# Self-attention of layer 3: the exponential ahead of the copies out of PSUM on ScalarE

## The reference

```python
q = jnp.einsum('bsc,hcd->bhsd', xn, wq)
k = jnp.einsum('btc,hcd->bhtd', yn, wk)
v = jnp.einsum('btc,hcd->bhtd', yn, wv)
a = jax.nn.softmax(jnp.einsum('bhsd,bhtd->bhst', q, k) * D ** (-0.5), axis=-1)
if causal:
    s, t = (a.shape[-2], a.shape[-1])
    mask = (jnp.arange(t)[None, :] > jnp.arange(s)[:, None]).astype(a.dtype)
    a = a * mask
o = jnp.einsum('bhst,bhtd->bhsd', a, v)
```

## Time and profile before

| | us |
|---|---|
| median of 3 runs | 2292.03 |
| lowest and highest run | 2288.86, 2292.82 |
| profiled execution, its own time | 2294.41 |
| its span in the trace | 2292.7 |
| PE, DVE, ACT, POOL busy over the span | 1993.1, 1211.0, 919.7, 537.7 |

### The profile page before, as it was taken

One profiled execution on the slowest core, in us unless ns is written; L12 is line 12 of the kernel. 1 busy time (PEld: TensorE's weight loads), 2 busy tenths in 40 slices (PEclk: granted clock), 3 DMA queues, 4 the chain that ended last, 5 costly groups with the idle time before them and its releaser, 6 DMA issues. The chain is left out here.

```text
span 2292.7 us, 33172 instructions
## 1 busy us (share of the span) xinstructions
PE 1993.1 (87%) x12069; PEld 1501.7 (65%) x12133; DVE 1211.0 (53%) x2415; ACT 919.7 (40%) x1811; POOL 537.7 (23%) x958
## 2 busy tenths in 40 slices
PE   5995995468878788999999979979989889999997
PEld 4663884354545555666666658855678678888897
DVE  4872223524862637888888844438724552332232
ACT  4221001212335557888888842323333242222232
POOL 0013222131002441222222223310123132222222
PEclk9997995668989899999999989989999999999999
DMA  2005441000002395444334030110000245556584
GB/s 96 1 1 178 127 135 50 14 14 16 1 1 33 103 241 128 93 93 93 93 93 93 11 109 19 21 49 1 1 15 1 69 168 176 163 172 193 165 272 172
DMA packets 169666, 198.90 MB, mean 87 GB/s; under 512 B 43627, under 2 KB 139906, under 8 KB 163360
## 3 DMA queue, kind: packets, MB, share of 16 engines
q1 hardware_dynamic: 157840, 183.67, 27.2%
q0 software_dynamic: 10944, 13.03, 2.9%
q10 hardware_dynamic: 720, 0.07, 0.0%
HBM read 162.45 MB, written 36.70 MB: 87 GB/s over the span
## 5 line engine op out<-in xcount | busy, mean ns | idle before, releaser
L2697 DVE TENSOR_REDUCE l3s_mx<-banks 128x1 f32<-128x1024 f32 x256 | 308.7, 1217 | 29.5 <-PE banks L2596 28.9
L1285 PE MATMUL banks<-l3f_xrt,l3f_w 128*128 128x256 f32 (+1 forms) x1536 | 275.5, 340 | 1.5 <-issue 1.5
L1285 PEld LDWEIGHTS banks<-l3f_xrt,l3f_w 128*128 128x128 f32 x1536 | 248.1, 191 | 26.9 <-issue 1.7
L2596 PE MATMUL banks<-l_stack 128*128 128x512 bf16 x960 | 249.8, 382 | 13.1 <-PEq L44 10.2
L1570 DVE TENSOR_SCALAR l3f_sg<-banks 128x256 f32<-128x256 f32 (+1 forms) x192 | 72.0, 375 | 280.3 <-PE banks L1285 280.3
L1352 ACT ACTIVATE l3f_sg<-l3f_sg 128x256 f32<-128x256 f32 (+1 forms) x192 | 72.5, 378 | 201.6 <-DVE l3f_sg L1570 201.6
L2688 ACT ACTIVATE x_features<-banks,l3s_mx 128x1024 f32<-128x1024 f32 x128 | 142.6, 1114 | 25.4 <-DVE l3s_mx L2697 23.7
L2596 PEld LDWEIGHTS banks<-l_stack 128*128 128x128 bf16 x1024 | 100.6, 98 | 78.4 <-issue 13.9
L2688 ACT ACTIVATE xn_tokens<-banks,l3s_mx 128x1024 f32<-128x1024 f32 x128 | 142.6, 1114 | 19.2 <-DVE l3s_mx L2697 19.1
L195 PE MATMUL banks<-ident,xn_tokens 128*128 128x128 f32 x320 | 60.7, 322 | 90.8 <-DVE xn_tokens L184 63.0
L1298 PE MATMUL banks<-l3f_w,l3f_ht 128*128 128x256 f32 x624 | 138.5, 379 | 0.0
(11 more groups left out here) (544 smaller groups left out, 3624.3 us busy)
## 6 DMA issues: line engine op xcount, KB each, us to landing
l3f_w<-in_L_ffn_gate_up_w_dram SPq DMA_DIRECT2D x24, 2048.0 KB, 8.5
l3f_w<-in_L_ffn_down_w_dram SPq DMA_DIRECT2D x24, 1024.0 KB
l0f_w<-in_L_ffn_W_dram SPq DMA_DIRECT2D x16, 1024.0 KB, 8.2
l_stack<-l_q_part SPq DMA_DIRECT2D x64, 256.0 KB, 5.9
l_stack<-l_k_part SPq DMA_DIRECT2D x64, 256.0 KB, 11.7
l_q_part<-l_stack SPq DMA_DIRECT2D x24, 256.0 KB, 3.2
l_k_part<-l_stack SPq DMA_DIRECT2D x24, 256.0 KB, 3.8
l_values<-l3p_vs SPq DMA_DIRECT2D x16, 256.0 KB, 3.7
```

Of the source, the lines that this page charges most:

```text
L1285: last = nc.tensor.matmul(ps[:, f % 4, h * PAIR:h * PAIR + size(t)], w1_sb[:, p, dc, h * FF + f * P:h * FF + (f + 1) * P], xrt[:, p, dc, 0 ...
L2596: last = nc.tensor.matmul(ps[:, 2 * (v % SCORES) + h, :], stack[p][0][s][:, r, si * P:(si + 1) * P], stack[p][1][s][:, r, h * 512:(h + 1) ...
L2697: nc.vector.tensor_reduce(mx[:, v % RING:v % RING + 1], ps[:, 2 * (v % SCORES):2 * (v % SCORES) + 2, :].rearrange("p a n -> p (a n)"), AX_ ...
```

## The change

On ACT a turn now begins with the exponential, and the copies of outputs and of transposes out of bank 6 follow it. Nothing is added or taken away, and no other engine's code changes.

```diff
             @block.scalar
             def _(act):
                 for v in range(ENTRIES * UNITS + OUT + 1):
-                    store_output(act, nc.scalar, v, 0)
-                    if v >= TURN:
-                        store_turned(act, nc.scalar, v - TURN, 0)
                     if v < ENTRIES * UNITS:
                         act.wait_ge(measured, v + 1)
                         if v >= RING:
@@ -2688,6 +2685,10 @@
                         nc.scalar.activation(ex[v % RING][:, :], ps[:, 2 * (v % SCORES):2 * (v % SCORES) + 2, :].rearrange("p a n -> p (a n)"),
                                              ACT.Exp, bias=mx[:, v % RING:v % RING + 1],
                                              accum_out=sm[:, v % RING:v % RING + 1]).then_inc(exped, 1)
+                    store_output(act, nc.scalar, v, 0)
+                    if v >= TURN:
+                        store_turned(act, nc.scalar, v - TURN, 0)
```

## The result

The changed kernel takes 2409.72 us (median of four runs, 2404.13 to 2410.97), the kernel before 2290.91 (four runs): a ratio of 1.0514 with a 95% interval of 1.0495 to 1.0533. It is slower by 119 us; 2411 was forecast.

A forecast was written before the change was run, and what follows sets the result against it. PE came first (busy 450.82 of the stage's 474 us), with ACT waiting for it and exponentials no one's limit. Entries of 15.07 us, eight of them less 1.6, gave 119 us on 2292: 2411, range 2370 to 2450.

The forecast's parts named there:

- three places: Points in eight turns where PE needs bank 6 sooner than ACT gives it; together 4.09 us in the first eight.
- the whole chain of the forecast: Bank 6 comes free at scores end + 0.03 + 1.22 + 0.03 + 1.10 + copy + 0.15 us.
- place 1: Fourth turn of the wide group (5 to 8 blocks): PE's transposes wait for bank 6, +1.60 us in the first eight turns.
- the give-back: A maximum that waited behind a DVE copy starts at once when PE is late: up to 0.26 us, 0.18 taken.
- The sum: Loss over the whole stage: 15.07 us an entry of 32 turns, eight entries, less 1.6: 119 us.
- hand-over of 0.15 us: Time from the end of a drain of bank 6 to PE's next transpose, read from 992.39 to 992.54.
- place 2: Output of the narrow group (1 to 4 blocks), on bank 6: starts later by +0.93 us in the first eight turns.
- place 3: First turn of the next wide group: second half of the transposes waits for bank 6, +1.56 us.
- PE's share: Sign that the forecast is right: PE busy near 76% of a stage that spans about 593 us.
- The clock rival: PE's holes of about 1.6 us lower the granted clock to 0.85: 2480 to 2547, say 2510 us; chance 0.08.
- The faster rival: ACT loses 39.5 us of idle time before copies and all comes back if exponentials set the pace: 2252; chance 0.03.

The follow-up runs named there:

- Single-place kernels: Kernel before, exponential first on ACT only in one turn of eight, the fourth wide, narrow-output or first wide one: 2340.84, 2311.52, 2335.34 us.
- the three together: Kernel before, exponential ahead of ACT's copies only in three turns of eight (96 of 256): 2407.13 us, ratio 1.0506.
- a second wide turn: Kernel before, exponential first on ACT only in the second turn of each wide group: 2295.17 us, ratio 1.0018.
- outputs alone: Kernel before, only ACT's copies of outputs moved behind the exponential, copies of transposes left ahead: 2311.35 us, ratio 1.0079.
- masks that were a turn older: Changed kernel with transposes four units behind the scores instead of three (TURN 4), outputs also a turn later: 2407.63 us, ratio 1.0502.

## Why the prediction was right

**The path.** At all three places PE waits for a bank that ACT copies out only after an exponential, as forecast. At places 2 and 3 the timeline shows the whole chain of the forecast: scores, maximum, exponential, copy, bank. At place 1 the chain has another start. In the third wide turn DVE copies an output ahead of the maximum and waits for PE with it; before the change already:

```profile
993.44 1.03 PE L2596 MATMUL banks<-l_stack 128*128 128x512 bf16 x4
...
995.78 0.42 DVE L2674 COPY l3s_raw<-banks 128x256 f32<-128x256 f32 x1 [1.56 <-PE banks L2629]
```

These scores end at 994.47. By the forecast's own chain PE could have written bank 6 again at 994.47 + 0.03 + 1.22 + 0.03 + 1.10 + 0.59 + 0.15 = 997.59, and it came to it at 997.61: no loss. The 1.60 us were right because they were counted from the exponential's start in the rows, which had DVE's late maximum in it. That DVE puts its maximum ahead of its copy, as the forecast says, holds for the copies of transposes only. So in this group of 8 blocks the price of place 1 needs both orders, ACT's and DVE's: the estimate from these rows is that it goes if DVE takes the maximum first. No run here tries that with the changed order on two banks.

Single-place kernels give 47, 21 and 42 us where the formulas of the forecast, with the hand-over of 0.05 us at places 2 and 3 that the next paragraph explains, give 53, 18 and 47 (32 places each, before what is given back). Places 1 and 3 fall short by 6 and 5 us, the three together by 1. Whether that is the give-back, which I had put at 0.18 to 0.26 us in eight turns, is not shown.

**The sum.** It was 119 us for the stage; the stage lost 115, the profiled spans differ by 116.6 and the medians by 118.8. An entry's 32 turns take 73.29 us, 14.46 more than before, where 15.07 more was forecast. Part of the close hit of the total is therefore the scatter of the runs, which is luck. The term that was mis-sized is the hand-over of 0.15 us from a copy's end to PE. At place 1 it is 1029.28 - 1029.14 = 0.14, but at place 2 it is 1033.93 - 1033.88 and at place 3 it is 1039.84 - 1039.79: 0.05 each. I had read it off one row where PE waits at the first transpose of a unit, and used it for all three places. With 0.05 place 2 would have been 3.73 (measured 3.75) and place 3 would have been 2.67 (2.69). 64 places by 0.1 us are 6 us: 113 instead of 119, against 115 measured.

**PE's share.** 76% was forecast, 466.18 of 588 us or 79% measured. Most of that is how the traces count: before, 960 of the 1024 score matmuls had a record (249.8 us), after all 1024 (263.9).

**What ACT has to spare.** ACT was 82% busy and is now 384.25 of 588, 65%, and the kernel is slower for its order alone. Read as a forecast, the Trainium skill's rule to look to the engine with the highest occupancy (Perfetto Trace Analysis, Identifying the Most-Contended Engine) gave no change; the runs differ from that by 119 us. The Trainium skill (Perfetto Trace Analysis, Optimization Strategy) then says to look for the gaps of the engine that is to be made faster and for what blocks it there. This trace agrees: PE's gaps end with ACT's copies, 108.5 us of them.

**The clock.** PE's holes at places 1 and 3 are 1.43 and 1.31 us, and the granted clock in the stage is 1.00. The clock rival fell. Its price in the forecast was too high as well: a stretch at a mean clock of 0.85 takes 1 / 0.85 = 1.18 times as long as at 1.00, not 1.30 times, so PE's 450.82 us would have grown by 80 us and not by 135, and the rival stood at 2451 to 2491. The Trainium skill's second failure mode (TensorE: Matmul & The Clock Gate, A second HAM failure mode: psum-queue depth-cycling), a clock that goes down and up with short idles from cycling through banks, does not show in this stage, whose granted clock is 1.00.

**The faster rival** was right in its first half: ACT did lose its 39.5 us before copies. It had no one to give them to.

**What I had missed.** That the outputs' copies have a price of 18 us that only shows alone, and that a second wide turn costs some 5 us. Neither moves the total. The outputs' copies lie behind place 2, as the rows above show. The second wide turn lies ahead of place 1, and there the later waits shrink: in the group of 7 blocks of the third entry PE of the changed kernel waits 0.34 us (at 1044.27) and then 1.31 at place 1 and 0.46 at place 2, where the kernel with the three turns alone has no such wait and then 1.54 and 0.67.

## What to carry to other kernels

When an engine drains a shared bank and also does work that depends on the newest product, put first what is ready first: here, at places 2 and 3, the copy can go while the exponential still waits for a maximum (1.22 us) to end. Look also at what stands ahead of that maximum on its own engine, as the output's copy does at place 1. Price a change of order by going along the waits of the buffer that is given back, use by use, not by the idle time of the engine whose order changes; that idle time (39.5 us here) can be the cover that keeps another engine going. And try the parts alone: prices of places in one loop do not add (18 us of outputs alone, none in the whole).

## What the runs showed of the hardware that was not expected

The gap from the end of ACT's copy to PE's next instruction was 0.14 to 0.15 us in the waits at place 1 and 0.04 to 0.06 us in nearly all of those at places 2 and 3 of the changed kernel. It is not a matter of beginning a unit: outputs that wait for DVE's copy start 0.14 to 0.15 us behind it, outputs that wait for ACT's 0.04 to 0.06. What sets it is not shown. And a wait row can name an engine that is not the cause: PE's weight loads stood 79.6 us "for masks" in the changed kernel, and 82.4 us with masks that were a turn older, while the time stayed the same to about a thousandth.
